# Wide attention: weights split inside the dense stage, normalisation moved into its own block; two order edits in the narrow attention

## The chip, the cores and the metric

The kernel runs on one core of a Trainium2 chip. The metric is the device time of one launch in microseconds. Three timed runs of the kernel before gave 2533.31, 2536.18 and 2537.85 us; their median is 2536.18 us. The engines are PE (TensorE, matmuls and transposes), DVE (VectorE), ACT (ScalarE), POOL (GpSimd) and SP (SyncE, which here only issues DMAs). Each engine executes its own instruction stream in order and meets the others at semaphores.

## The reference, cut to what matters

The program is a chain of eight sub-layers on `x` (16 batches, 112 tokens, 256 channels) with a context of 375 tokens per batch. Each one normalises the rows and adds its result to `x`: narrow attention (16 heads of 16), a top-1 expert layer, linear attention, a dense mixture of 8 small experts, **wide attention** (16 heads of 64), a top-2 expert layer, narrow attention again, a last expert layer. The layernorm and the wide attention, sub-layer 4, in essence:

```python
xn = (x - mean(x)) / sqrt(var(x) + 1e-5)             # over the 256 channels
q = xn @ Wq                                           # 256 -> 16 heads x 64
k, v = ctx @ Wk, ctx @ Wv                             # 375 context tokens
s = (q k^T) / sqrt(64), masked by the context mask
y = softmax(s) v                                      # per head
x = x + (y @ Wo + bo)
```

`k` and `v` depend on the context and the weights alone, `q` on the normalised rows.

## The kernel before, in words

Each sub-layer is a phase. A phase has one or more blocks; a block gives each engine its own instruction list, and all engines meet at the block's end. When a phase gives back its memory object (`Mem`, L31), its semaphores are cleared and there is a barrier of all engines (L39 to L43).

**Precision.** Most matmuls are made in three fp16 products (`PARTS`, L25): each operand is a high part (a cast of the value) and a low part (value minus high part). ACT makes the high parts; DVE or POOL the low ones. "Splitting" below means making both.

**Layernorm** (`layernorm_phase`, L91 to L206) is a block of its own. For four groups of four batches, DVE makes statistics (`bn_stats`, `bn_aggr`), ACT the root, DVE the reciprocal and the shift; ACT normalises rows 0 to 9, DVE rows 10 to 15; PE transposes (32 transposes, 112 x 128) into eight banks; ACT and DVE copy to `XT`, the transposed rows. Its SP list can fetch something for the next block (`fetch`), its POOL list can prepare something (`prepare`).

**Dense stage** (`dense_ffn_phase`, L1615 to L1874). After the routing, 32 units (8 experts x 4 groups of batches) follow. Per unit PE makes 12 output matmuls (L1844) and 6 hidden matmuls (L1824) of the unit four further on; ACT makes the gelu (L1725) and the high part of the hidden values (L1730), POOL the low part (L1686), DVE four additions to X (L1808). At every fourth unit ACT and DVE also split the weights of an expert (L1695, L1696, L1752, L1755). The output banks are four, one per batch of the group, and PE waits before each for the addition of the unit before.

**Wide attention** (`wide_attention_phase`, L209 to L649). Its layernorm's SP list fetches `Wk`, the context of batch 0, `Wq`, `Wv`, the context of batch 1, two masks, `Wo` and the bias (L287 to L296), into the room that the values use later (`staged`). Its POOL list splits `Wk` in three operations on 128 x 2048 (`prepare`, L298 to L304). After the layernorm's end a second block begins. Its lists start with a prologue: ACT makes the high parts of context 0, `Wq`, the rows of group 0, `Wv`, context 1 (L433 to L438), DVE the low parts of `Wq`, the rows, `Wv` (L527 to L533), POOL the low parts of the contexts and two masks (L356 to L360). Then come steps s from -3 to 132. Step s scores head pair s (L609), turns the weights of pair s - 2 (L619) and weighs the values of pair s - 3 (L635); 128 pairs in all. Between these lie the projection units of a step (`units_at`): keys `k` (6 matmuls, L572), queries `q` (L579), values `v` (L586), outputs (L595). They go through two banks in turn; a unit waits until the one two before it was emptied by DVE (L566). Steps -3 to -1 hold k, q and v units of batch 0; scoring starts at step 0.

**Narrow attention** (`narrow_attention_phase`, L652 to L1100), used by sub-layers 0 and 6; only in sub-layer 6 are there `v` units. All its projection units share ONE bank, so each waits until the one before was emptied (L1062). Per batch of 8 steps there are k (2), v (3), the turn of the maxima, `turn_y` (L1093, emptied by a reciprocal and a multiplication on DVE, L967 and L969), `turn_n` (L1096) and `out`. `units_at` (L666) lists the units of a step by batch. So in the step where `turn_y` of batch b and the second v unit of batch b + 2 meet, `turn_y` comes first. The SP list issues per batch the stacked keys, the maxima (L820), the context, and for each group of four batches the stacked queries (L813) at steps 8b - 20 and 8b - 12.

## Time and profile before

| what | value |
|---|---|
| timed runs, median | 2536.18 us |
| profiled execution, its own time | 2536.97 us |
| its span in the trace | 2535.3 us |
| mean granted clock of PE over the span | 0.921 |
| PE busy | 2168.5 us, 86% |
| DVE, ACT, POOL busy | 62%, 55%, 38% |

The trace's times begin at the span's start. The profiled execution's own time is 1.67 us above its span, and 0.79 us above the median of the timed runs. A row of a timeline begins with its start and its length in microseconds; the square bracket at its end is the idle time of that engine before it and the instruction that ended it.

### The profile page before, as it was taken

How to read it: one execution, taken by the hardware profiler on the slowest of the kernel's cores; microseconds unless marked ns; L12 is line 12 of the kernel's file. 1: busy time of each engine (PE TensorE's matmuls, PEld its weight loads, DVE VectorE, ACT ScalarE, POOL GpSimd, SP SyncE). 2: the span in 40 equal slices, each digit the busy share in tenths (PEclk: the TensorE clock that was granted, in tenths of full speed). 3: DMA queues.
4: the chain of work that ended last, by engine and by line, in shares of the span. 5: the costliest groups of instructions: out<-in, count | busy, mean ns of one | idle time of the engine just before them, and what ended most of it. 6: DMA issues, size and time to landing. Idle time of an engine off the chain costs nothing. (4 is left out here: it accounts for less than half of the span.)

```text
span 2535.3 us, 62742 instructions
## 1 busy us (share of the span) xinstructions
PE 2168.5 (86%) x24002; PEld 1469.8 (58%) x24002; DVE 1563.0 (62%) x3645; ACT 1402.4 (55%) x3000; POOL 969.5 (38%) x1069
## 2 busy tenths in 40 slices
PE   4999499599999999969699999999974975899755
PEld 2566256367777777747456666666652642566533
DVE  3667673576566556647777777777756544655463
ACT  3666563455555555535466666666654543666542
POOL 3553232154454445424423333333333733433143
PEclk8999699799999999989799999999987985999968
DMA  5663361400000000010200000000023233332133
GB/s 124 122 115 75 101 233 38 128 14 14 14 8 14 14 14 2 2 35 1 96 7 15 9 15 14 9 15 8 2 86 107 74 94 95 85 75 70 42 102 111
DMA packets 118583, 139.60 MB, mean 55 GB/s; under 512 B 15073, under 2 KB 107185, under 8 KB 118289
## 3 DMA queue, kind: packets, MB, share of 16 engines
q1 hardware_dynamic: 110900, 115.39, 17.6%
q0 software_dynamic: 7392, 20.19, 2.5%
q8 instruction: 200, 3.28, 0.5%
q14 instruction: 91, 0.74, 0.1%
HBM read 93.25 MB, written 17.47 MB: 44 GB/s over the span
## 5 line engine op out<-in xcount | busy, mean ns | idle before, releaser
L952 DVE TENSOR_REDUCE a_mx<-a_pair 112x2 f32<-112x750 f32 x256 | 238.0, 937 | 191.1 <-PE a_pair L1021 191.1
L1260 POOL TENSOR_TENSOR a_kp<-a_kp 125x512 f16<-125x512 f32 x192 | 217.6, 1157 | 259.4 <-ACT a_kp L1351 259.4
L353 POOL TENSOR_SCALAR a_P<-a_P,a_inv 112x375 f32<-112x375 f32 x256 | 148.4, 593 | 379.6 <-DVE a_inv L484 379.6
L391 ACT ACTIVATE a_P<-a_masked,a_least 112x375 f32<-112x375 f32 x256 | 153.4, 600 | 141.0 <-DVE a_least L479 141.0
L890 ACT ACTIVATE a_PT<-a_pair 125x672 f32<-125x672 f32 x256 | 186.2, 730 | 65.3 <-PE a_pair L1033 60.9
L479 DVE CUSTOM_DVE_ANT_0 a_masked<-a_s,a_mask_add 112x375 f32<-112x375 f32 x256 | 130.2, 547 | 81.7 <-PE a_s L609 79.4
L1394 DVE SCALAR_TENSOR_TENSOR a_k<-a_p,a_k 128x375 f16<-128x375 f32 x128 | 69.3, 547 | 139.2 <-ACT a_k L1307 139.1
L1351 ACT CAST a_kp<-a_kp 125x512 f16<-125x512 f32 x192 | 110.3, 617 | 76.9 <-DVE a_kp L1413 76.9
L572 PE MATMUL a_p<-a_kc,a_wk 128*128 128x375 f16 x768 | 146.2, 326 | 4.3 <-POOL a_kc L347 4.3
L586 PE MATMUL a_p<-a_wv,a_kc 128*125 128x512 f16 x576 | 144.6, 387 | 5.2 <-DVE a_v L518 3.7
L1493 PE MATMUL a_p<-a_kc,a_wk 128*128 128x375 f16 x768 | 142.2, 327 | 6.3 <-POOL a_kc L1252 6.3
L1493 PE MATMUL a_p<-a_wv,a_kc 128*125 128x512 f16 x576 | 141.0, 385 | 0.0
L2327 PE MATMUL f_hb<-w_w1h,f_x 128*128 x588 | 135.7, 367 | 0.0
L2415 ACT ACTIVATE all_XT<-f_hb 128x512 f32<-128x512 f32 (+1 forms) x98 | 53.1, 550 | 138.8 <-PE f_hb L2327 130.5
L1413 DVE TENSOR_SCALAR a_kp<-a_p 125x512 f32<-125x512 f32 x192 | 122.8, 682 | 8.1 <-PE a_p L1524 8.1
L619 PE MATMUL a_t<-all_ident,a_P 112*125 112x112 f32 x768 | 116.4, 288 | 3.4 <-POOL a_P L353 3.4
L489 DVE TENSOR_TENSOR a_PT<-a_t,a_PT 125x336 f16<-125x336 f32 x256 | 116.8, 498 | 2.6 <-ACT a_PT L427 2.6
L619 PEld LDWEIGHTS a_t<-all_ident,a_P 112*125 112x125 f32 x768 | 93.7, 188 | 38.9 <-issue 34.6
L586 PEld LDWEIGHTS a_p<-a_wv,a_kc 128*125 128x125 f16 x576 | 71.4, 137 | 61.4 <-DVE a_v L518 15.3
L1052 PE MATMUL a_y<-a_PT,a_values 125*32 125x112 f32 x3072 | 101.5, 265 | 5.3 <-ACT a_PT L890 5.3
L1403 DVE SCALAR_TENSOR_TENSOR a_v<-a_p,a_v 125x512 f16<-125x512 f32 x96 | 66.6, 694 | 58.4 <-ACT a_v L1318 56.8
L1033 PE MATMUL a_pair<-a_q,a_k 50*125 50x112 f16 (+1 forms) x1536 | 89.0, 223 | 15.0 <-DVE a_mx L952 8.6
(450 smaller groups left out, 5366.7 us busy)
## 6 DMA issues: line engine op xcount, KB each, us to landing
a_kc<-in_ctxT SPq DMA_DIRECT2D x64, 375.0 KB, 3.6
a_k<-a_k_parts SPq DMA_DIRECT2D x192, 93.8 KB
w_stage<-in_L_ffn_W SPq DMA_DIRECT2D x32, 512.0 KB
w_stage<-in_L_ffn_ew SPq DMA_DIRECT2D x16, 512.0 KB, 6.9
w_stage<-expert_rows SPq DMA_DIRECT2D x16, 448.0 KB, 8.1
a_v_in_sb<-in_ctx SPq DMA_DIRECT2D x16, 375.0 KB
a_q<-a_q_parts SPq DMA_DIRECT2D x48, 112.0 KB, 4.6
w_stage<-in_L_ffn_W SPq DMA_DIRECT2D x16, 256.0 KB, 4.5
```

Of the source, the lines that this page charges most:

```text
L353: pool.tensor_scalar(P[:, p % 4, r, :], P[:, p % 4, r, :], inv[:, p % 4, r:r + 1], 1.0, ALU.mult, ALU.mult).then_inc(P_done, 1)
L391: act.activation(P[:, p % 4, r, :], masked[:, p % 2, r, :], ACT.Exp, bias=least[:, p % 4, r:r + 1], scale=-1.0, accum_out=total[:, p % 4, ...
L479: dve.tensor_tensor_reduce(masked[:, p % 2, r, :], s_bank[0:S, r, 0:SK], mask_add[:, b % 2, :], 1.0, 3e38, ALU.add, ALU.min, least[:, p % ...
L572: mm = pe.matmul(out[:, 0:SK], wk16[:, z, j, c * 128:(c + 1) * 128], kc16[:, b % 2, x, j, :], start=i == j == 0, stop=(i, j) == (2, DC - 1))
L586: mm = pe.matmul(out[0:KP, 0:512], kc16[:, b % 2, x, j, jk * KP:(jk + 1) * KP], wv16[:, z, j, w * 512:(w + 1) * 512], start=i == j == 0, s ...
L619: mm = pe.transpose(t_bank[0:KP, r, j * S:(j + 1) * S], P[:, p % 4, r, j * KP:(j + 1) * KP], ident[0:S, 0:S])
L890: act.activation(PT[:, p % 4, :, :], pair_bank[slot["turned", p]][0:KP, :, 0:KT * S], ACT.Exp).then_inc(exp_done, 1)
L952: dve.tensor_reduce(mx[:, b % 2, 2 * pair:2 * pair + 2], pair_bank[slot["score", p]][0:S, :, 0:SK], AX.X, ALU.max).then_inc(max_done, 1)
L1260: pool.tensor_tensor(kp16[:, LO, j, hf, r, :, :].rearrange("p c m -> p (c m)"), kp[:, n % 4, :], kp16[:, HI, j, hf, r, :, :].rearrange("p ...
L1413: dve.tensor_scalar(kp[:, n % 4, :], p_bank[bank][0:KP, 0:512], 0.0, EPS * WS, ALU.max, ALU.add).then_inc(f_evac, 1)
L1493: mm = pe.matmul(out, lhs(x, z, j), rhs(x, z, j), start=i == j == 0, stop=(i, j) == (2, DC - 1))
L2327: mm = pe.matmul(bank[:, 0:BW], x16[:, j % 2, x, c, :], w.w1h[:, z, c, bass.ds(e, 1), cols].rearrange("p o f -> p (o f)"), start=False, st ...
```

## The change

- A new class `WideWeights` holds the wide attention's weight and context tiles. It is made before the dense stage, and the dense stage's second block has an SP list that issues their five DMAs. From unit 6 to unit 17 of the dense stage, ACT makes one high part and DVE one low part per unit, each 128 x 512 (12 pieces: three matrices, two chunks, two halves). At units 20 and 22 they split the contexts of batches 0 and 1.
- The wide attention has no layernorm block any more, and POOL's `prepare` and the prologue on POOL, ACT and DVE for weights and contexts are gone. A class `Normalised` carries out the layernorm within the block's steps, which now start at -9: keys 0, 1, 2 of batch 0 are projected at steps -9, -8, -7, values at -6, -5, -4, queries at -3, -2, -1. ACT normalises groups 0 and 1, DVE groups 2 and 3. The transposes use the score, turn and value banks. SP issues the masks, `Wo` and the bias at the block's start.
- Narrow attention: v units come first in their step; the stacked queries are issued at steps 8b - 22 and 8b - 14.
- There is one block less in the program, and as many `Mem` objects with semaphores as before; one is now given back at the end of the wide attention.

```diff
+class Normalised:
+    def statistics(self, dve, g):
+        for b in range(g * GT, (g + 1) * GT):
+            dve.bn_stats(self.stats[:, b, :], self.X[:, b, :]).then_inc(self.stats_done, 1)
...
+    def normalise_dve(self, dve, g):
+        dve.wait_ge(self.rstd_done, g + 1)
+        for b in range(g * GT, (g + 1) * GT):
+            dve.tensor_scalar(self.xn[:, b, :], self.X[:, b, :], self.mean_var[:, b, 0:1], self.rstd[:, b:b + 1],
+                              ALU.subtract, ALU.mult).then_inc(self.dve_rows, 1)
...
+    def normalise_act(self, act, g):
+        act.wait_ge(self.shift_done, g + 1)
...
+    def take_act(self, act, g, c, place):
+        act.wait_ge(self.turned, place + 1)
+        act.copy(self.XT[:, c, g * GW:(g + 1) * GW], self.banks[g][c][:, 0:GW]).then_inc(self.act_taken, 1)
+    def turn(self, pe, g, rows_done, count):
+        pe.wait_ge(rows_done, count)
+        for c in range(DC):
+            for t in range(GT):
+                mm = pe.transpose(self.banks[g][c][:, t * S:(t + 1) * S], self.xn[:, g * GT + t, c * 128:(c + 1) * 128],
+                                  self.ident[0:S, 0:S])
+            mm.then_inc(self.turned, 1)
...
+class WideWeights:
+    PIECES = [(w, c, h) for w in ("k", "q", "v") for c in range(DC) for h in range(2)]
...
+    def fetch(self, sp):
+        for w in ("k", "q", "v"):
+            sp.dma_start(self.staged[w], chunked(self.given[w])).then_inc(self.w_in[w], 16)
+        for b in range(2):
+            self.load_context(sp, b)
+    def high(self, act, i):
+        w, c, h = self.PIECES[i]
+        cols = slice(h * 512, (h + 1) * 512)
+        act.wait_ge(self.w_in[w], 16)
+        act.mul(self.w16[w][:, HI, c, cols], self.staged[w][:, c, cols], WS).then_inc(self.w_hi, 1)
+    def low(self, dve, i):
...
+        dve.wait_ge(self.w_hi, i + 1)
+        dve.scalar_tensor_tensor(self.w16[w][:, LO, c, cols], self.staged[w][:, c, cols], WS, self.w16[w][:, HI, c, cols],
+                                 ALU.mult, ALU.subtract).then_inc(self.w_split, 1)
...
# wide attention
-    FIRST, LAST = -3, NPAIR + WEIGH + 1
+    FIRST, LAST = -9, NPAIR + WEIGH + 1
-    V_FIRST = {-3: (0, 0), -1: (1, 0), 1: (2, 0), 2: (0, 1), 3: (1, 1), 4: (2, 1)}
+    K_FIRST = {-9: 0, -8: 1, -7: 2}
+    V_FIRST = {-6: (0, 0), -5: (1, 0), -4: (2, 0), 2: (0, 1), 3: (1, 1), 4: (2, 1)}
...
-        layernorm_phase(nc, tag + "n", X, XT, ident, fetch=fetch, prepare=prepare)
...
# ACT's list, before the units of step s
+                    if s == -8:
+                        norm.root(act, 0)
+                    if s == -7:
+                        norm.root(act, 1)
+                        norm.normalise_act(act, 0)
+                    if s == -6:
+                        norm.root(act, 2)
+                        norm.normalise_act(act, 1)
+                        norm.root(act, 3)
+                        for c in range(DC):
+                            norm.take_act(act, 0, c, c)
+                        high_x(0)
+                    if s == -4:
+                        for c in range(DC):
+                            norm.take_act(act, 1, c, DC + c)
+                    if s == -2:
+                        norm.take_act(act, 2, 0, 2 * DC)
+                    if s == -1:
+                        norm.take_act(act, 3, 0, 3 * DC)
...
# DVE's list, before the emptying of step s - 1's last unit
+                    if -8 <= s <= -6:
+                        g = s + 9
+                        norm.statistics(dve, g)
+                        norm.invert(dve, g - 1)
+                        norm.aggregate(dve, g)
+                        norm.shifts(dve, g - 1)
+                    if s == -5:
+                        norm.normalise_dve(dve, 2)
+                        low_x(0)
+                    if s == -4:
+                        norm.invert(dve, 3)
+                        norm.normalise_dve(dve, 3)
+                    if s == -2:
+                        norm.take_dve(dve, 2, 1, 2 * DC + 1)
+                    if s == -1:
+                        norm.take_dve(dve, 3, 1, 3 * DC + 1)
...
# PE's list, before the units of step s
+                    if s == -5:
+                        norm.turn(pe, 0, norm.act_rows, GT)
+                    if s == -4:
+                        norm.turn(pe, 1, norm.act_rows, 2 * GT)
+                    if s == -3:
+                        norm.turn(pe, 2, norm.dve_rows, GT)
+                    if s == -2:
+                        pe.wait_ge(norm.act_taken, 4)
+                        norm.turn(pe, 3, norm.dve_rows, 2 * GT)
...
# narrow attention
-        return found
+        return [u for u in found if u[0] == "v"] + [u for u in found if u[0] != "v"]
...
-                        if t in (-20, -12) and b % GT == 0:
-                            stack_queries(b // GT, (t + 20) // 8)
+                        if t in (-22, -14) and b % GT == 0:
+                            stack_queries(b // GT, (t + 22) // 8)
...
# dense stage, ACT and DVE at unit n
+                    if 6 <= n < 6 + len(following.PIECES):
+                        following.high(act, n - 6)
+                    if n in CONTEXT_AT:
+                        following.high_context(act, CONTEXT_AT.index(n))
...
+                    if kind == "unit" and 6 <= n < 6 + len(following.PIECES):
+                        following.low(dve, n - 6)
+                    if kind == "unit" and n in CONTEXT_AT:
+                        following.low_context(dve, CONTEXT_AT.index(n))
```

## Rows read from the trace of the kernel before

**Rows 1.** The page's parts 1 and 2: PE's share of the span, and its granted clock.

```profile
PE 2168.5 (86%) x24002; PEld 1469.8 (58%) x24002; DVE 1563.0 (62%) x3645; ACT 1402.4 (55%) x3000; POOL 969.5 (38%) x1069
...
PEclk8999699799999999989799999999987985999968
```

**Rows 2.** Busy us of engines by stretch: dense units, layernorm, prologue, steps; `PEclk` is the clock.

```profile
1146.00:1229.00 83.00, 81.46 (x592) 63.66 (x590) 62.26 (x154) 37.24 (x69) 34.05 (x30) 0.98 0.00 1
1229.00:1251.00 22.00, 9.30 (x32) 5.58 (x32) 20.08 (x48) 10.26 (x22) 11.34 (x3) 0.57 0.68 236
1251.00:1272.00 21.00, 14.52 (x55) 6.32 (x56) 11.11 (x10) 10.09 (x13) 7.40 (x4) 0.64 0.13 41
1272.00:1860.00 588.00, 579.69 (x5627) 380.53 (x5626) 432.30 (x1210) 399.81 (x1068) 197.62 (x300) 1.00 0.04 10
```

**Rows 3.** Timeline of PE from the prologue to step 0.

```profile
1254.15 2.04 PE L572 MATMUL a_p<-a_kc,a_wk 128*128 128x375 f16 x6 [4.27 <-POOL a_kc L347]
...
1267.55 1.14 PE L572 MATMUL a_p<-a_kc,a_wk 128*128 128x375 f16 x6
...
1271.36 0.69 PE L609 MATMUL a_s<-a_k,a_q 64*112 64x375 f16 x6
...
```

**Rows 4.** Timeline of DVE over the same stretch.

```profile
1214.75 1.66 DVE L1808 SCALAR_TENSOR_TENSOR all_X<-f_o,f_scaled,all_X 112x256 f32<-112x256 f32 x4 [0.79 <-PE f_o L1844]
...
1229.64 1.41 DVE L126 BATCH_NORM_STATS2 a4n_stats<-all_X 112x6 f32<-112x256 f32 x4
...
1239.62 3.89 DVE L145 TENSOR_SCALAR a4n_xn<-all_X,a4n_mean_var,a4n_rstd 112x256 f32<-112x256 f32 x2
...
1254.16 2.56 DVE L528 SCALAR_TENSOR_TENSOR a_wq<-a_v,a_wq 128x2048 f16<-128x2048 f32 x1 [3.62 <-ACT a_wq L435]
1256.65 1.08 DVE L468 TENSOR_TENSOR a_x<-all_XT,a_x 128x896 f16<-128x896 f32 x1
...
```

**Rows 5.** Timeline of ACT and of POOL over the same stretch.

```profile
1233.40 2.06 ACT L168 ACTIVATE a4n_xn<-all_X,a4n_shift,a4n_rstd 112x256 f32<-112x256 f32 x4
...
1252.22 1.91 ACT L435 ACTIVATE a_wq<-a_v 128x2048 f16<-128x2048 f32 x1
...
1209.09 1.55 POOL L1686 TENSOR_TENSOR f_h<-f_h 128x448 f16<-128x448 f32 x1 [1.41 <-ACT f_h L1730]
...
1236.02 5.39 POOL L300 TENSOR_SCALAR a_v<-a_v 128x2048 f32<-128x2048 f32 x1 [11.22 <-DMA a_v<-in_L_xattn_Wk]
...
```

**Rows 6.** DVE's groups in the dense stage's layernorm: count, busy us, mean ns.

```profile
L145 DVE TENSOR_SCALAR f3n_xn<-all_X,f_mean_var,f_rstd 112x256 f32<-112x256 f32 x6 | 2.1, 410 | 0.0
L131 DVE BATCH_NORM_AGGREGATE f_mean_var<-f3n_stats 112x2 f32<-112x6 f32 x16 | 1.5, 157 | 0.0
```

**Rows 7.** Timelines of DVE and POOL at the head of the dense stage.

```profile
1128.19 1.82 DVE L1752 SCALAR_TENSOR_TENSOR f_w1h<-f_w,f_w1h 128x256 f16<-128x256 f32 x1 [0.95 <-ACT f_w1h L1695]
...
1127.85 7.96 POOL L1682 TENSOR_TENSOR f_x<-all_XT,f_x 128x896 f16<-128x896 f32 x4 [22.94 <-ACT f_x L1692]
```

**Rows 8.** DVE at two phase ends: the last bracket is the gap between phases.

```profile
1870.61 0.06 DVE L148 MEMSET q5n_eps<- 112x1 f32 x1 [1.28 <-PEq L43]
...
2101.92 0.06 DVE L148 MEMSET a6n_eps<- 112x1 f32 x1 [2.57 <-PEq L43]
```

**Rows 9.** Timeline of PE in sub-layer 6: turn_y, the v unit behind it, and a q unit.

```profile
2255.63 0.65 PE L1093 MATMUL a_p<-all_ident,a_y_sb 128*112 128x128 f32 x4
2257.11 0.87 PE L1082 MATMUL a_p<-a_wv,a_kc 128*125 128x256 f16 x6 [0.83 <-DVE a_yn L969]
...
2266.28 1.77 PE L1076 MATMUL a_p<-all_XT,a_wq 128*128 128x448 f32 x4 [0.47 <-ACT a_values L918]
...
```

**Rows 10.** Waits of sub-layer 6: us in total, times, longest.

```profile
PE a_p L1082 <- DVE a_yn L969: 11.7, 14, 0.8
```

**Rows 11.** Timeline of SP's queue in sub-layer 6: context, then queries.

```profile
2235.51 0.40 SPq L735 DMA_DIRECT2D a_kc<-in_ctxT  x1
2236.01 2.75 SPq L813 DMA_DIRECT2D a_q<-a_q_parts  x3
...
```

More of the change, by code:

```diff
@@ L211, in wide_attention_phase @@
+def wide_attention_phase(nc, tag, X, XT, ident, given, Wo, bo, mask):
     HD, NP = 64, H // 2
@@ L226, in units_at @@
             t = s - NP * b
-            found += [("k", b, t + 3)] if 0 <= t + 3 < C else []
+            if b == 0:
+                found += [("k", 0, K_FIRST[t])] if t in K_FIRST else [("k", 0, t + 3)] if 0 <= t < C - 3 else []
+            else:
+                found += [("k", b, t + 3)] if 0 <= t + 3 < C else []
             if b == 0:
@@ L326, in _ @@
             def _(sp):
+                for b in range(2):
+                    load_mask(sp, b)
+                sp.dma_start(wo, chunked(Wo)).then_inc(rest_in, 16)
+                sp.dma_start(bo_bc[:, :], bo.unsqueeze(0).to_broadcast([S, D])).then_inc(rest_in, 16)
                 for s in steps:
@@ L331, in _ @@
                             sp.wait_ge(kc_split, b - 1)
-                            load_context(sp, b)
+                            given.load_context(sp, b)
                         if t == -12:
@@ L567, in project @@
                     if kind == "k":
-                        pe.wait_ge(wk_split, 1)
+                        pe.wait_ge(given.w_split, 4)
                         pe.wait_ge(kc_split, b + 1)
@@ L606, in score @@
                         pe.wait_ge(least_done, 2 * p)
+                    else:
+                        pe.wait_ge(norm.act_taken, 2)
                     for i, (x, z) in enumerate(PARTS):
@@ L617, in turn @@
                             pe.wait_ge(PT_done, 2 * (p - 1) + r + 1)
+                        else:
+                            pe.wait_ge(norm.act_taken, 6)
+                            pe.wait_ge(norm.dve_taken, 2)
                         for j in range(KT):
@@ L1677, in dense_ffn_phase, with _ @@
         with nc.Block() as block:
+            @block.sync
+            def _(sp):
+                following.fetch(sp)
             @block.gpsimd
@@ L2684, in sub7, with sub34 @@
                        a["L3_ffn_Wg"], bias=a["L3_ffn_bg"], out=out)
+        def sub34():
+            with ExitStack() as st2:
+                wide = WideWeights(Mem(nc, st2, "w4"), a["ctxT"], a["L2_xattn_Wq"], a["L2_xattn_Wk"], a["L2_xattn_Wv"])
+                sub3(wide)
+                sub4(wide)
         first_sub, stop = stop if isinstance(stop, tuple) else (0, stop)
-        for sub in (sub0, sub1, sub2, sub3, sub4, sub5, sub6, sub7)[first_sub:stop]:
+        for sub in (sub0, sub1, sub2, sub34, sub5, sub6, sub7)[first_sub:stop]:
             sub()
```

139 lines of the change are left out of this document (83 added, 56 removed).

## The prediction

> **What bounds the kernel now.** I read the page first, then a table by stretch, then the timelines of each engine between the dense stage and the wide attention. PE is busy for 86% of the span, and the page's slices show its clock at 9 or more nearly everywhere except at a few phase changes [rows 1]. The table shows which these are: in the dense units PE works 81.46 of 83 us at a clock of 0.98 and in the wide steps 579.69 of 588 us at 1.00, but between them lie 43 us with PE busy for 9.30 of 22 and 14.52 of 21 us, at 0.57 and 0.64, that is mostly at the lower of its two levels, 1.2 and not 2.4 GHz [rows 2]. So the change can win nothing in the steady steps except by taking work out of them; it can win in the 43 us, and it pays in the dense units, where PE is the bound as well.
>
> What fills the 43 us: the layernorm begins at 1229.64 [rows 4] and the first score comes at 1271.36 [rows 3], 41.7 us later. In the layernorm DVE is the late engine (20.08 busy of 22 us [rows 2]): two normalisations took 3.89 us [rows 4] where the same six took 2.1 us together, 0.35 each, in the dense stage's layernorm, in which POOL did nothing [rows 6]. Beside the slow ones POOL worked 5.39 us on Wk [rows 5]. Then the prologue: PE waits 4.27 us for a context's low part before its first key unit [rows 3], and DVE spends 2.56 us on Wq after waiting 3.62 us for its high part, the same again on Wv, and 1.08 us on the rows [rows 4].
>
> **The lead-in, step by step.** Call the new block's start 0; it is at 1229.6, as before, if the dense stage ends when it did. Keys and values need no row of x, so PE starts at once. DVE's list decides until step -4. Statistics take 1.41 us per group [rows 4] and aggregates 1.5 / 4 = 0.38 [rows 6], 7.2 us for four groups; three key units are emptied between them (0.5 each, from 2.56 us for 2048 columns [rows 4]), and reciprocals and shifts add some 0.4: 9.1 us. Group 2 is normalised in 4 x 0.35 [rows 6]: 10.5. The low part of the rows comes next and needs, in a row, eight transposes, two copies and a high part on ACT. ACT has normalised groups 0 and 1 by about 9 us (2.06 us each [rows 5], the second after DVE's second shift at 6.2); the chain then puts the high part at 11 to 13.5 and the low part (1.08 [rows 4]) at 12.2 to 14.5. A value unit, group 3 and another value unit on DVE (0.65 + 1.4 + 0.65) give 15 to 17. After that PE has two transposes of groups and three query units, each waiting for the unit two before.
>
> PE itself has 3 key, 3 value and 3 query units and four groups of transposes. At the low clock a key unit takes 2.04 us, at the high one 1.14 [rows 3]; by columns a query unit is 2.44 or 1.36, a value unit 2.79 or 1.56; a group of transposes is 9.30 / 4 = 2.3 us at the low clock [rows 2], half of it at the high. The sum is 31 us at the low clock and 16.5 at the high. So the first score is at about 21 if PE stays fast (DVE and the handovers are the bound) and at 31 if it stays slow (PE is). At the low clock PE would have no gaps, and in the prologue of before it went from 2.04 to 1.14 us for the same unit after a few us without gaps [rows 3]. I take 23, near the fast end. The gain is 41.7 - 23 = 18.7 us, with ends 10.7 and 20.7.
>
> At the first score all of before's lead-in units are done, and one value unit more (the third, step 1 before). It leaves the steps where PE is the bound: 6 products by the column rule, 1.5 us, less some overlap: 1.4.
>
> **The dense units.** A unit lasts 1.66 + 0.79 = 2.45 us, of which DVE is idle 0.79 [rows 4]. A low piece of 512 columns is a quarter of the 2.56 us for 2048 [rows 4], about 0.68 with its fixed part, so it fits: 1.66 + 0.68 = 2.34. At units 6, 10 and 14 the expert's weights are split too (about 0.8); DVE falls behind by 0.7 each and recovers 0.1 per unit, at most 1.7 us. PE waits for an addition only when it comes to the same bank again, a unit later, which leaves 1.5 to 2 us. ACT's high piece is a quarter of 1.91 us [rows 5], 0.5 to 0.6, on an engine that works 37.24 of 83 us [rows 2]. The DMAs are issued some 35 us before unit 6; nothing else loads in that stage (1 GB/s, the last column of [rows 2]). Taken: 0.5 us lost, with ends 0 and 15. The far end is for DVE and POOL holding each other up. At the stage's head one 256-wide DVE split, with both inputs in SBUF, took 1.82 us while POOL's operations ran, 7.96 us for four [rows 7]. In the units it went the other way: DVE's split began first, and POOL's low part, next to it, took 1.55 us [rows 5], which PE does not feel, as that unit's output is 1 to 2 units away. New pieces stand at the place of those splits, right behind the additions, so I take the cheap order.
>
> The Trainium skill (SBUF — State Buffer, section "SBUF: two separate sides") says that DVE with two SBUF inputs and GpSimd share one port pair, that whoever starts first keeps it for the whole instruction, and that the other blocks. Both rows agree. By that rule the dense stage is a lottery of some 0.1 us in starts; if POOL won each time, the far end holds (it is a rival below).
>
> **The ends of phases.** One gap between blocks goes with the layernorm; it is inside the 41.7 us. One more memory object is given back at the wide attention's end. A phase end with one such object shows a gap of 1.28 us, one with three 2.57 [rows 8]: 0.65 each. Taken: +0.65, ends 0.3 and 1.3.
>
> **Narrow attention.** In sub-layer 6 PE waits 14 times 0.83 us, 11.7 in all, between turn_y and the value unit behind it, as both use the one bank and DVE must first take its two steps [rows 9, 10]. With the value unit first, turn_y waits for ACT instead; that handover shows 0.47 us before a query unit [rows 9]. DVE's two steps then lie beside the score, the turned score and the weighing of the next step, over 1 us of PE's work, before turn_n asks for them. 14 x (0.83 - 0.47) = 5.0 us; at the last two or three batches DVE's maxima are late as well, so 4.6, with ends 0 and 6. Sub-layer 0 has no value units. The queries: SP issues them directly behind the context anyway (2235.51, 2236.01 [rows 11]), so moving them up two steps mostly swaps these two. What is queued behind them on SP, the keys, is not ready then, and the context is wanted ten steps later. Where they wait for a free buffer SP waits longer, but no longer than to the same point. Taken: 0, within 1 either way.
>
> **The sum.** -18.7 - 1.4 + 0.5 + 0.65 - 4.6 = -23.6 us. From the profiled execution's own time, 2536.97, that gives 2513.4; on the scale of the median, 0.8 lower, 2512.6. I predict 2513.
>
> **Rivals.**
> 1. *PE stays slow in the lead-in.* For: the clock is at its lower level in the layernorm and until some 37 us after its start [rows 2, 3], and new gaps between units could keep it there. Against: at that level there are no gaps. First score at 31: 8 us less won, 2521. Chance 0.13.
> 2. *POOL wins the port in the dense units.* Each of 12 pieces then costs 1.0 us more, 1.66 + 0.68 + 1.03 (POOL's length without a wait: 1.55 less half a us) - 2.45 = 0.9, with weights and contexts 15: 2527. Chance 0.07. If each piece is held for as long as at the stage's head (1.82 for 256 columns [rows 7], so 2.1 for 512), it is 12 x (1.66 + 2.1 - 2.45) = 16, the six weight splits 6 x 1.4 = 8, two contexts 5: 29 lost in place of 0.5, and the kernel is slower, 2541. It decides from 24 us lost. Against: beside the split in the units it was POOL that was held, not DVE [rows 5]. Chance 0.03.
> 3. *The narrow order wins nothing*, because ACT's handover comes behind an exponential, or the maxima become the bound: 2518. Chance 0.15.
> 4. *More is won*: the lead-in ends at 20, DVE's chain loses its handovers, narrow gives 6: 2507. Chance 0.12.
> The forecast has the other 0.50.
>
> **How the numbers follow.** All but the slow branch of the second are faster by more than 5 us, which is the 0.2% that this kernel's measurement can tell. Range: 2505 to 2523 takes in the first, third and fourth, and leaves out 2527 and 2541 and the tails. Faster 0.95, within 0.2% 0.02, slower 0.03.
>
> **What would show it.** The first score should come 21 to 25 us after the dense stage's end gap, key units at once, DVE without pieces over 2 us in the statistics. The dense units should keep 2.45 us, with no PE idle on DVE's additions beyond 1 us. In sub-layer 6 the 0.83 us waits should be gone and 14 of about 0.47 us stand before turn_y; the wait in front of turn_n should not appear. The steps of the wide attention keep their pace. Wrong would be: PE at 2.04 us per key unit up to step 0; unit lengths of 3 us from unit 6 to 17; a new wait of a maximum in sub-layer 6.

## The result, and the profile after

The changed kernel takes 2510.47 us (median of 4 runs, 2509.68 to 2512.50) where the kernel before takes 2536.11 (4 runs, 2533.31 to 2537.85). The ratio is 0.9896, with a 95% interval of 0.9881 to 0.9911: 26 us faster, between 23 and 30. The prediction said 2513, in a range from 2505 to 2523. The profiled execution took 2512.50 us, with a span of 2510.8, 24.5 less than before's 2535.3.

The page's parts 1 and 2 after, against [rows 1]: PE, DVE and POOL are busy for 8 to 10 us less. The 20th digit of the clock, the slice that holds the lead-in of the wide attention, is 9 where it was 7.

```profile
PE 2160.3 (86%) x24002; PEld 1468.2 (58%) x24002; DVE 1554.1 (62%) x3659; ACT 1403.2 (56%) x3008; POOL 959.8 (38%) x1064
...
PEclk8899789899999999988999999999986995999867
```

**Where the time went.** I cut the trace at the first instruction of each sub-layer's layernorm (DVE's memset of `eps`) and measured the stages, here for before, after and the whole-program kernels of the experiments below. In us:

```
                       sub 0   sub 1   sub 2  dense 3  wide 4   sub 5   sub 6   sub 7    span
before                 260.6   213.6   625.7   118.4   641.0   231.3   297.9   135.5   2535.3
after                  267.9   213.7   625.2   118.5   618.0   228.5   292.3   135.3   2510.8
changed_again          262.6   212.7   627.6   117.1   619.0   232.3   290.5   133.0   2506.8
e1_old_queries         259.3   211.9   625.4   118.5   618.0   227.8   291.7   120.2   2484.6
e2_old_values          268.0   213.8   625.2   118.5   617.9   228.6   296.4   120.7   2500.6
e3_narrow_only         267.8   211.4   625.7   118.4   642.0   230.3   293.6   121.1   2521.6
e4_wide_only           261.8   212.1   627.3   117.0   618.9   228.0   296.5   122.0   2495.5
e5_dense_split         260.2   212.3   627.5   117.1   625.3   230.8   294.4   120.6   2499.8
e7_pool_first          268.7   213.3   624.6   117.8   618.1   228.1   296.6   134.5   2513.6
e8_context_first       269.1   212.7   627.5   117.1   619.0   227.8   291.9   135.6   2512.3
e9_context_late        267.9   214.9   625.4   118.9   618.3   228.7   292.3   133.0   2510.7
```

After minus before: the wide attention -23.0, sub-layer 6 -5.6, sub-layer 5 (no code changed) -2.8, **sub-layer 0 +7.3**, the other four -0.5 together. The table tells also what one profile is worth: sub-layers 1, 2 and 5, whose code is the same in every kernel, spread by 3 to 4.5 us (sub-layer 5: 227.8 to 232.3). The wide stage with its new lead-in agrees within 1.1 us (617.9 to 619.0). One of the 12 runs of e3_narrow_only took 2552.92 us at a granted clock of 0.879 and stands in none of its figures below.

**The lead-in.** Engines by stretch after, against [rows 2]: dense units, the lead-in's two halves, steps. The columns are those of [rows 2].

```profile
1153.00:1236.00 83.00, 81.47 (x592) 63.71 (x590) 70.42 (x168) 44.78 (x83) 42.96 (x31) 0.98 0.00 1
1236.70:1246.60 9.90, 6.81 (x33) 4.01 (x34) 9.75 (x46) 7.80 (x18) 2.35 (x2) 0.83 0.66 214
1246.60:1256.50 9.90, 8.59 (x57) 5.60 (x57) 6.65 (x13) 6.02 (x12) 0.00 (x0) 1.00 0.00 1
1256.50:1845.00 588.50, 580.26 (x5631) 381.48 (x5631) 432.55 (x1211) 400.02 (x1067) 197.61 (x300) 1.00 0.04 10
```

The 43 us of before with PE at 0.57 and 0.64 are now 19.8 us. In the first half DVE is busy for 9.75 of 9.90 us, so it is the bound there; in the second half it is PE, at full clock. PE's timeline, against [rows 3]:

```profile
1236.82 2.09 PE L720 MATMUL a_p<-w_kc,w_wk 128*128 128x375 f16 x12 [2.35 <-PEq L43]
...
1240.79 1.14 PE L720 MATMUL a_p<-w_kc,w_wk 128*128 128x375 f16 x6 [1.88 <-DVE a_k L645]
1243.02 2.82 PE L734 MATMUL a_p<-w_wv,w_kc 128*125 128x512 f16 x6 [1.09 <-DVE a_k L645]
...
1246.53 1.46 PE L734 MATMUL a_p<-w_wv,w_kc 128*125 128x512 f16 x6
...
1250.06 1.51 PE L734 MATMUL a_p<-w_wv,w_kc 128*125 128x512 f16 x6 [1.31 <-DVE w_v L654]
...
1254.08 2.44 PE L727 MATMUL a_p<-a_x,w_wq 128*128 128x448 f16 x12
1256.45 0.69 PE L759 MATMUL a_s<-a_k,a_q 64*112 64x375 f16 x6
```

Two key units take 2.09 us together right at the block's start, the high level (1.14 for one in [rows 3]); only one value unit, 2.82 against 1.46, ran at the low level; and PE's idle brackets name DVE's emptying. DVE's timeline, against [rows 4]:

```profile
1236.70 1.41 DVE L231 BATCH_NORM_STATS2 a_stats<-all_X 112x6 f32<-112x256 f32 x4
...
1245.11 1.37 DVE L254 TENSOR_SCALAR a_space<-all_X,a_mean_var,a_rstd 112x256 f32<-112x256 f32 x4
...
1248.31 1.09 DVE L604 TENSOR_TENSOR a_x<-all_XT,a_x 128x896 f16<-128x896 f32 x1 [1.83 <-ACT a_x L506]
...
1250.13 1.38 DVE L254 TENSOR_SCALAR a_space<-all_X,a_mean_var,a_rstd 112x256 f32<-112x256 f32 x4
```

The block begins at 1236.70 and the first score is at 1256.45: 19.75 us, where before took 41.7. Four normalisations take 1.37 us, 0.34 each, where two had taken 3.89 beside POOL. In before that row has two neighbours that were slow as well, while POOL worked on Wk: a shift that takes 0.13 us here, and four more normalisations.

```profile
1236.63 3.07 DVE L139 SCALAR_TENSOR_TENSOR a4n_shift<-a4n_mean_var,a4n_rstd 112x4 f32<-112x4 f32 x1
...
1243.64 4.99 DVE L145 TENSOR_SCALAR a4n_xn<-all_X,a4n_mean_var,a4n_rstd 112x256 f32<-112x256 f32 x4
```

From the first score to the next layernorm's memset it is 598.20 us, where before had 1870.61 - 1271.36 = 599.25.

**The dense units.** DVE and then POOL around unit 6, against [rows 4, 5]:

```profile
1177.21 0.42 DVE L1926 SCALAR_TENSOR_TENSOR f_w2h<-f_w,f_w2h 128x256 f16<-128x256 f32 x1
1177.55 0.69 DVE L335 SCALAR_TENSOR_TENSOR w_wk<-w_v,w_wk 128x512 f16<-128x512 f32 x1
1178.15 1.66 DVE L1979 SCALAR_TENSOR_TENSOR all_X<-f_o,f_scaled,all_X 112x256 f32<-112x256 f32 x4
...
1185.08 1.66 DVE L1979 SCALAR_TENSOR_TENSOR all_X<-f_o,f_scaled,all_X 112x256 f32<-112x256 f32 x4 [0.19 <-PE f_o L2019]
```

```profile
1176.98 2.15 POOL L1853 TENSOR_TENSOR f_h<-f_h 128x448 f16<-128x448 f32 x1 [1.41 <-ACT f_h L1897]
...
1179.43 1.88 POOL L1853 TENSOR_TENSOR f_h<-f_h 128x448 f16<-128x448 f32 x1 [0.29 <-ACT f_h L1897]
```

DVE's piece takes 0.69 us; it is POOL's low part that is held, 2.15 us in this unit and 1.88, 1.60 and 1.48 in the next three. The same four lengths come back, within 0.01 us, in the units from 10 and from 14. PE's only wait for DVE from 1150 to 1236 us was this one (us in total, times, longest), and the stage kept its length, 118.4 to 118.5.

```profile
PE f_o L2016 <- DVE f_gT L1967: 1.3, 1, 1.3
```

**The end of the wide phase,** against the first of [rows 8]: the gap with one more object given back is 1.75 us for 1.28. The second gap of [rows 8], where nothing was changed, is 2.1 us after for 2.57 before, so a single gap tells the price of an object only within half a us.

```profile
1854.65 0.06 DVE L148 MEMSET q5n_eps<- 112x1 f32 x1 [1.75 <-PEq L43]
```

**Sub-layer 6.** The wait of [rows 10] is gone. In its place (first fence: waits), and on PE's timeline, against [rows 9]:

```profile
PE a_p L1255 <- ACT a_values L1080: 6.6, 14, 0.5
```

```profile
2233.67 0.87 PE L1244 MATMUL a_p<-a_wv,a_kc 128*125 128x256 f16 x6
2235.02 0.65 PE L1255 MATMUL a_p<-all_ident,a_y_sb 128*112 128x128 f32 x4 [0.48 <-ACT a_values L1080]
2236.06 0.78 PE L1214 MATMUL a_y<-a_PT,a_values 125*32 125x112 f32 x24
2236.77 0.41 PE L1258 MATMUL a_p<-all_ident,a_yn 112*128 112x112 f32 x2
```

14 waits of 0.83 us became 14 of 0.47, and turn_n follows with no wait before it.

**Sub-layer 0.** This is where the profile contradicts the prediction. SP's queue, first before, then after (start, us to issue):

```profile
116.62 0.29 SPq L738 DMA_DIRECT2D a_v_in_sb<-in_ctx  x1
116.95 0.54 SPq L735 DMA_DIRECT2D a_kc<-in_ctxT  x1
119.11 1.89 SPq L813 DMA_DIRECT2D a_q<-a_q_parts  x3
...
```

```profile
122.71 0.29 SPq L900 DMA_DIRECT2D a_v_in_sb<-in_ctx  x1
125.19 1.88 SPq L975 DMA_DIRECT2D a_q<-a_q_parts  x3
127.11 1.80 SPq L897 DMA_DIRECT2D a_kc<-in_ctxT  x1
129.01 3.79 SPq L962 DMA_DIRECT2D a_k<-a_k_parts  x6
```

The queries issue no earlier than they did: 2.49 us after the values (`v_in_sb`) before, 2.48 after, because SP waits 2.1 us for their free buffer (L973). The context, now behind them, comes 4.40 us after the values and not 0.33, so it is 4.1 us late. Of the sub-layer's six pairs two are so; in the other four the context is 1.9 to 2.0 us late, the time that the queries take to issue.

PE's waits for the maxima, which come over the same queue, in the sub-layer before and after:

```profile
PE a_pair L1033 <- DMA a_q<-a_mT: 6.3, 5, 2.0
```

```profile
PE a_pair L1195 <- DMA a_q<-a_mT: 10.5, 6, 3.4
```

4.2 us more stand in that line. They can't be the whole account of the 7.3: PE is also busy for 219.9 us in this stage where it was 215.4, with the same 2992 matmuls, at a granted clock of 0.89 for 0.92. Whether the moved queries did it, and by how much, a single pair of profiles can't say; most of the experiments are about that.

### The profile page after: what moved, and what is told of

The parts are those of the page before. It is cut to its first block and busy times, and to the rows that moved or that the text cites. A ratio compares the mean times of both kernels' runs of the same rounds, so it can differ in the third digit from the quotient of the medians.

```text
span 2510.8 us, 62752 instructions
## 1 busy us (share of the span) xinstructions
PE 2160.3 (86%) x24002; PEld 1468.2 (58%) x24002; DVE 1554.1 (62%) x3659; ACT 1403.2 (56%) x3008; POOL 959.8 (38%) x1064
## 5 line engine op out<-in xcount | busy, mean ns | idle before, releaser
L475 POOL TENSOR_SCALAR a_space<-a_space,a_inv 112x375 f32<-112x375 f32 x256 | 148.4, 593 | 384.0 <-DVE a_inv L620 384.0
L513 ACT ACTIVATE a_space<-a_space,a_least 112x375 f32<-112x375 f32 x256 | 153.4, 600 | 141.1 <-DVE a_least L615 141.1
L615 DVE CUSTOM_DVE_ANT_0 a_space<-a_s,a_mask_add 112x375 f32<-112x375 f32 x256 | 130.2, 547 | 81.7 <-PE a_s L759 79.3
L734 PE MATMUL a_p<-w_wv,w_kc 128*125 128x512 f16 x576 | 144.6, 387 | 6.1 <-DVE w_v L654 5.0
L720 PE MATMUL a_p<-w_kc,w_wk 128*128 128x375 f16 x768 | 144.3, 323 | 4.2 <-PEq L43 2.3
L1655 PE MATMUL a_p<-a_kc,a_wk 128*128 128x375 f16 x768 | 142.2, 326 | 6.3 <-POOL a_kc L1414 6.3
L1655 PE MATMUL a_p<-a_wv,a_kc 128*125 128x512 f16 x576 | 141.0, 385 | 0.0
L2502 PE MATMUL f_hb<-w_w1h,f_x 128*128 x588 | 135.6, 367 | 0.0
L772 PE MATMUL a_t<-all_ident,a_space 112*125 112x112 f32 x768 | 116.3, 288 | 3.4 <-POOL a_space L475 3.4
L772 PEld LDWEIGHTS a_t<-all_ident,a_space 112*125 112x125 f32 x768 | 93.5, 188 | 38.9 <-issue 34.3
L734 PEld LDWEIGHTS a_p<-w_wv,w_kc 128*125 128x125 f16 x576 | 71.3, 137 | 61.7 <-DVE w_v L654 16.8
```

The costliest lines, as they stand in the source:

```text
L475: pool.tensor_scalar(P[:, p % 4, r, :], P[:, p % 4, r, :], inv[:, p % 4, r:r + 1], 1.0, ALU.mult, ALU.mult).then_inc(P_done, 1)
L513: act.activation(P[:, p % 4, r, :], masked[:, p % 2, r, :], ACT.Exp, bias=least[:, p % 4, r:r + 1], scale=-1.0, accum_out=total[:, p % 4, ...
L615: dve.tensor_tensor_reduce(masked[:, p % 2, r, :], s_bank[0:S, r, 0:SK], mask_add[:, b % 2, :], 1.0, 3e38, ALU.add, ALU.min, least[:, p % ...
L720: mm = pe.matmul(out[:, 0:SK], wk16[:, z, j, c * 128:(c + 1) * 128], kc16[:, b % 2, x, j, :], start=i == j == 0, stop=(i, j) == (2, DC - 1))
L734: mm = pe.matmul(out[0:KP, 0:512], kc16[:, b % 2, x, j, jk * KP:(jk + 1) * KP], wv16[:, z, j, w * 512:(w + 1) * 512], start=i == j == 0, s ...
L772: mm = pe.transpose(t_bank[0:KP, r, j * S:(j + 1) * S], P[:, p % 4, r, j * KP:(j + 1) * KP], ident[0:S, 0:S])
```

## The experiments

Each kernel was timed beside the kernel before on the same chip, and ratios are to it. Absolute times differ from chip to chip (below), so they are compared only among kernels timed together.

### One part at a time

**The changed kernel with the queries back at their old steps:**

```diff
-                        if t in (-22, -14) and b % GT == 0:
-                            stack_queries(b // GT, (t + 22) // 8)
+                        if t in (-20, -12) and b % GT == 0:
+                            stack_queries(b // GT, (t + 20) // 8)
```

> The changed kernel with the stacked queries issued at steps 8b - 20 and 8b - 12 again. Sub-layer 0, from the start of its layernorm (11.4) to that of the next, took 260.6 us in the kernel before and 267.9 in the changed one, though only this edit touches it. Theory A, the moved queries cost it: they go ahead of a context and push what follows on SP's queue, the maxima land later. Then sub-layer 0 is back at about 261 us and the kernel at about 2504. Rival B, the landing of the DMAs varies from one execution to the next: sub-layer 0 lies anywhere in 260 to 268 here, and the kernel is at 2510 within 2 us.

Measured: 2491.06 us (2486.35 to 2497.59), before 2525.98; ratio 0.9874 (0.9851 to 0.9897). Sub-layer 0 took 259.3 us, sub-layer 6 291.7.

**The changed kernel with the value units back in their old order:**

```diff
-        return [u for u in found if u[0] == "v"] + [u for u in found if u[0] != "v"]
+        return found
```

> The changed kernel with the units of a narrow step in their old order (values not first), queries moved. Theory: PE waits 14 times 0.83 us behind turn_y again; sub-layer 6, 292.3 us in the changed kernel from its layernorm's start to the next one's, takes 297 to 298, and the kernel 2515 to 2516. Rival: the 5.6 us came from the moved queries or from chance, and the kernel stays at 2510 to 2511. Sub-layer 0, by theory A of the first run, is at about 268, by B anywhere in 260 to 268.

Measured: 2505.34 us (2497.90 to 2507.65); ratio 0.9920 (0.9899 to 0.9942). Sub-layer 6 took 296.4 us, sub-layer 0 268.0.

**Before with both narrow edits and nothing else** (the two diffs above turned round, on the kernel before):

> The kernel before with both edits of the narrow attention and none of the wide. By the prediction's terms it gains 4.6 us: 2531.5. By the traces, sub-layer 6 gains 5.6 and, by theory A, sub-layer 0 loses 7: 2537 to 2538. By rival B sub-layer 0 is unchanged on the mean: 2530.5.

Measured: 2523.80 us (2520.68 to 2528.70); ratio 1.0008 (0.9986 to 1.0031), between 4 us faster and 8 slower. The 4.6 us that the prediction's terms give are outside, though sub-layer 6 took 293.6 us in place of 297.9. Sub-layer 0 took 267.8.

**The wide attention's and the dense stage's edits alone** (both narrow edits undone, as in the two diffs):

> The changed kernel with both narrow edits undone: the wide and dense edits alone. By the prediction's terms 19.0 us faster than before, 2517. By the traces, where the stretch from the wide layernorm's start to the next layernorm went from 641.0 to 618.0 us and the dense stage stayed (118.4 and 118.5), 23 us: 2513. Both narrow parts together are then this kernel less the changed one: 2 to 3 us if the 23 hold, 6 to 7 if the 19 do.

Measured: 2497.95 us (2493.79 to 2503.21); ratio 0.9895 (0.9873 to 0.9916). Wide stage 618.9 us, dense 117.0.

What follows from the four, all from one chip: by the medians the wide and dense edits give 28.0 us, the value order 6.9 (2497.95 - 2491.06), and the moved queries cost 7.4 (2505.34 - 2497.95). By the ratios it is 26.5, 5.3 and 6.3. The last two have intervals of about 8 us each way, so only their signs are suggested. The value order has a better measure in the table: sub-layer 6 took 292.0 us in the mean of the six profiles that have it (290.5 to 293.6) and 296.4 in the five that don't (294.4 to 297.9), 4.3 less. And it shows that the queries do nothing in sub-layer 6: 291.7 with the old steps, 292.3 and 290.5 with the new.

### Why moved queries should cost anything

Two kernels were meant to tell the early queries from the late context. **Queries moved, but behind the context of the same step:**

```diff
                         if t == -11:
                             stack_keys(b)
-                        if t in (-22, -14) and b % GT == 0:
-                            stack_queries(b // GT, (t + 22) // 8)
...
                             load_context(sp, b)
+                    for b in range(0, B, GT):
+                        t = s - 8 * b
+                        if t in (-22, -14):
+                            stack_queries(b // GT, (t + 22) // 8)
```

> The changed kernel with the queries still at steps 8b - 22 and 8b - 14, but behind the context of the same step on SP's queue. Sub-layer 0 took 267.8 to 268.0 us in the three kernels with the queries moved and 259.3 to 261.8 in the three without. Theory C: the harm is that the moved queries stand ahead of a context, which then comes late and is moved when the maxima want to land. Then sub-layer 0 is back at 260 to 262 us and the kernel 7 us below the changed one. Rival D: the early queries themselves crowd the DMA queues behind the maxima; sub-layer 0 stays at 268.

Measured: 2511.21 us (2505.24 to 2518.28), before 2539.80; ratio 0.9894 (0.9858 to 0.9929). Sub-layer 0 took 269.1 us, as the rival had it and not the theory.

**Old query steps, the context at 8b - 28, behind them:**

```diff
-                        if t in (-22, -14) and b % GT == 0:
-                            stack_queries(b // GT, (t + 22) // 8)
+                        if t in (-20, -12) and b % GT == 0:
+                            stack_queries(b // GT, (t + 20) // 8)
...
-                        if t == -30 and b >= 3:
+                        if t == -28 and b >= 3:
```

> The changed kernel with the queries at their old steps and the context two steps later (8b - 28), so that it stands behind them on SP's queue and ahead of the keys. Theory C: a late context alone does the harm, sub-layer 0 at 267 to 268 us. Rival D: the queries are where they were, sub-layer 0 at 260 to 262.

Measured: 2514.19 us (2512.43 to 2520.29); ratio 0.9916 (0.9886 to 0.9945). Sub-layer 0 took 267.9 us.

**The changed kernel itself, on the same chip:**

> The changed kernel itself, as the reference on the same chip for the other kernels: sub-layer 0 at 268 us, the stretch from the wide attention's start to the next layernorm at 618, sub-layer 6 at 292, 1.0 to 1.1% faster than before.

Measured: 2509.12 us (2508.52 to 2510.25); ratio 0.9889 (0.9862 to 0.9916). Sub-layer 0 took 262.6 us here, where the same kernel had taken 267.9.

**These two kernels can't tell theory C from rival D.** A step is a place in SP's list and not a time: SP issues its list in order and waits only for what each entry needs. The context stands at steps 8b - 30, and no entry lies between it and the queries' old place two steps on. So "queries moved, but behind the context" is the list with the old query steps over again, entry by entry, and "old query steps, context later" is the changed kernel's. SP's queue in the first shows it, 2.16 us from the context to the queries as in before:

```profile
119.43 0.55 SPq L897 DMA_DIRECT2D a_kc<-in_ctxT  x1
121.59 1.89 SPq L975 DMA_DIRECT2D a_q<-a_q_parts  x3
```

The intervals of the three kernels overlap. What the two are good for is repetition. With the old order sub-layer 0 took 260.6, 259.3, 261.8, 260.2, 268.7 and 269.1 us (before, e1, e4, e5, e7, e8), with the new one 267.9, 262.6, 268.0, 267.8 and 267.9 (after, changed_again, e2, e3, e9): means of 263.3 and 266.8, and either order with short and long passes. A single profile of sub-layer 0 tells nothing of an effect below 8 us. So the sub-layer was repeated.

**Sub-layer 0 six times over, and nothing else of the program but the first load and the last store of X**, in three versions: old query steps; moved; moved but behind the context, which by the above is the first over again. The other sub-layers are left out, so what these kernels write is not the program's output.

```diff
-        for sub in (sub0, sub1, sub2, sub34, sub5, sub6, sub7)[first_sub:stop]:
-            sub()
+        for i in range(6):
+            narrow_attention_phase(nc, "n" + "abcdef"[i], X, XT, ident, a["ctxT"], a["L0_WqT"], a["L0_WkT"], a["L0_WcT"],
+                                   a["L0_xattn_bc"], a["L0_bq"], a["L0_bk"], ctx=a["ctx_1024"])
...
```

> Sub-layer 0 alone, carried out six times in a row (weights and context of sub-layer 0 each time), and X written out; the other sub-layers are left out. Queries at the old steps 8b - 20 and 8b - 12. In whole kernels sub-layer 0 with the old steps took 260.6, 261.8, 259.3 and once 268.7 us, with the moved ones 267.8 to 269.1 and once 262.6, so one profile does not tell. Theory A (the moved queries cost 5 to 7 us per sub-layer): this kernel lies 30 to 42 us below the one with moved queries, near 1585 against 1620. Rival B (chance from one execution to the next): both within 6 us of each other, and single sub-layers in one profile spread over 259 to 269.

> The same six sub-layers with the queries at 8b - 22 and 8b - 14, ahead of the step's context. Theory A: six times 5 to 7 us more than with the old steps. Rival B: the same within 6 us.

> The same six sub-layers with the moved queries behind the context of their step. If it is the displaced context that costs (theory C), this lies at the kernel with the old steps; if the moved queries themselves (D), at the one with moved queries. By rival B all three agree within 6 us.

| version | median, us | from, to | ratio to before, interval |
|---|---|---|---|
| old steps | 1602.30 | 1595.10, 1610.17 | 0.6347 (0.6328 to 0.6365) |
| moved | 1619.28 | 1608.94, 1628.62 | 0.6413 (0.6389 to 0.6437) |
| moved, behind the context (the old order again) | 1602.31 | 1592.72, 1611.34 | 0.6339 (0.6318 to 0.6361) |

Six moved sub-layers cost 17 us (from the intervals of the ratios, 9 to 25), 2.8 us each (1.5 to 4). The first and the third version, which issue the same list, agree within 0.01 us in their medians; their ten runs lie between 1592.72 and 1611.34 us, those of the new order between 1608.94 and 1628.62, and only two of the ten are above the lowest of those six. So the edit's price is real, it comes of the exchange of context and queries on the queue, which is all that the edit does there, and it is less than half of the 7.3 us that the first profile showed. Whether the early queries or the late context cost it, no run tells.

By which instruction it makes itself felt stays open. The waits for the maxima, which had seemed to be it, come to 48.1 and 51.9 us over the six sub-layers in the profiles of the old order, and to 55.1 in that of the new; the largest of a single sub-layer is alike (old steps, moved):

```profile
PE na_pair L1195 <- DMA na_q<-na_mT: 10.7, 5, 4.0
```

```profile
PE nc_pair L1195 <- DMA nc_q<-nc_mT: 10.7, 5, 3.8
```

More stands in PE's busy time, for the same number of matmuls (old steps, moved, moved behind the context):

```profile
PE 1306.4 (82%) x17952; PEld 825.5 (52%) x17952; DVE 910.2 (57%) x1548; ACT 920.0 (58%) x1536; POOL 647.4 (41%) x793
```

```profile
PE 1318.8 (82%) x17952; PEld 834.9 (52%) x17952; DVE 910.8 (56%) x1548; ACT 920.8 (57%) x1536; POOL 647.7 (40%) x793
```

```profile
PE 1310.6 (82%) x17952; PEld 829.8 (52%) x17952; DVE 910.5 (57%) x1548; ACT 921.3 (57%) x1536; POOL 648.3 (40%) x793
```

The spans of these three profiles are 1596.5, 1613.9 and 1603.9 us, the granted clocks 0.888, 0.881 and 0.891. Of the 13.7 us between the moved version and the mean of the other two, 10.3 are PE's busy time. So the exchange seems to cost mainly by a lower clock and less by PE's waits, as far as one profile of each tells.

And equal sub-layers of one kernel differ by more than the effect: the second begins at 274.8 us in the profile of the version with the old steps, the third at 539.0, the fourth at 808.1, the fifth at 1066.4: 264.2, 269.1 and 258.3 us.

### The lead-in: splitting elsewhere, or normalising beside

**Weights split in the dense stage, but the layernorm in a block of its own and the steps from -3 as before** (the narrow edits undone):

```diff
-    FIRST, LAST = -9, NPAIR + WEIGH + 1
+    FIRST, LAST = -3, NPAIR + WEIGH + 1
-    K_FIRST = {-9: 0, -8: 1, -7: 2}
-    V_FIRST = {-6: (0, 0), -5: (1, 0), -4: (2, 0), 2: (0, 1), 3: (1, 1), 4: (2, 1)}
+    V_FIRST = {-3: (0, 0), -1: (1, 0), 1: (2, 0), 2: (0, 1), 3: (1, 1), 4: (2, 1)}
...
+        layernorm_phase(nc, tag + "n", X, XT, ident, fetch=fetch)
```

> Narrow edits undone; weights and contexts are split in the dense stage, but the wide attention keeps its own layernorm block (without POOL's work in it) and its steps from -3. It tells how the 22 us of the lead-in share out. Theory: the layernorm block takes 12.7 us as in the dense stage instead of 20.9, the prologue only the rows of group 0, so the first score comes some 26 us after the layernorm's start (41.7 before, 19.8 in the changed kernel): 15 to 16 us of the 22 belong to the split, 6 to 7 to the overlap. From the wide layernorm's start to the next one 624 to 626 us. Rival: the layernorm stays near 20 us also without POOL's work and the split alone brings under 10 us.

Measured: 2509.59 us (2501.51 to 2513.53), before 2526.66; ratio 0.9936 (0.9922 to 0.9949). The wide stage took 625.3 us, between 641.0 and 618.0. DVE's and then PE's timeline of this kernel:

```profile
1228.72 1.40 DVE L126 BATCH_NORM_STATS2 a4n_stats<-all_X 112x6 f32<-112x256 f32 x4
...
1235.76 0.73 DVE L145 TENSOR_SCALAR a4n_xn<-all_X,a4n_mean_var,a4n_rstd 112x256 f32<-112x256 f32 x2
```

```profile
1233.12 7.87 PE L204 MATMUL a4n_b<-all_ident,a4n_xn 112*128 112x112 f32 x32 [6.63 <-ACT a4n_xn L168]
1242.77 2.04 PE L677 MATMUL a_p<-w_kc,w_wk 128*128 128x375 f16 x6 [1.78 <-PEq L43]
...
1254.40 0.68 PE L714 MATMUL a_s<-a_k,a_q 64*112 64x375 f16 x6
```

From the layernorm's start to the first score it is 1254.40 - 1228.72 = 25.7 us: 16.0 of the 22.0 us won come from taking the splits out of the lead-in, 6 from laying the layernorm beside the projections. The pair of normalisations takes 0.73 us without POOL beside it, 3.89 with it [rows 4]. With the shift before it (0.13 us for 3.07) and the four behind it (1.38 for 4.99) these seven operations of DVE are 9.7 us shorter, so most of the 16.0 lies where DVE had worked beside POOL's splits of Wk. And here, with PE idle for 6.63 us first, the first key unit runs at 2.04 us, the low level.

### Who wins the port in the dense units

**The wide edits alone, and in units 6 to 17 DVE waits until POOL has been given its low part, so that POOL begins first;** two tiny memsets on DVE are added for the order:

```diff
                     if kind == "unit" and 6 <= n < 6 + len(following.PIECES):
+                        dve.wait_ge(h_hi, n + 4)
+                        for c in range(2):
+                            dve.memset(tick[:, n - 6, c, :], 0.0)
                         following.low(dve, n - 6)
```

> The kernel with the wide edits alone (narrow edits undone), and in units 6 to 17 of the dense stage DVE waits until POOL's low part has been released, makes two tiny memsets and only then its weight piece. So POOL starts first each time. By the rule of the shared port pair (second rival of the prediction) DVE is then held for POOL's 1.03 us before each of the 12 pieces: 1.66 + 0.2 + 1.03 + 0.68 = 3.6 us of DVE per unit against 2.45 of PE, 12 to 14 us more in the dense stage (118.4 to about 131 from its layernorm's start to the wide block's). If DVE is not held, DVE needs 2.6 us per unit and the stage gains 2 to 3 us (121).

Measured: 2513.71 us (2508.14 to 2515.30), before 2539.80; ratio 0.9898 (0.9869 to 0.9927). The dense stage kept its length, 117.8 us. DVE's pieces of 512 columns and POOL's low part in this kernel:

```profile
1176.47 1.48 DVE L335 SCALAR_TENSOR_TENSOR w_wk<-w_v,w_wk 128x512 f16<-128x512 f32 x1
...
1179.49 0.67 DVE L335 SCALAR_TENSOR_TENSOR w_wk<-w_v,w_wk 128x512 f16<-128x512 f32 x1
```

```profile
1175.85 1.54 POOL L1854 TENSOR_TENSOR f_h<-f_h 128x448 f16<-128x448 f32 x1 [1.41 <-ACT f_h L1898]
...
1178.30 1.04 POOL L1854 TENSOR_TENSOR f_h<-f_h 128x448 f16<-128x448 f32 x1 [0.90 <-ACT f_h L1898]
```

The first piece, begun after POOL's operation, took 1.48 us in place of 0.69; the second 0.67; six later ones 0.73 or 0.91. All 12 took 9.8 us, 8.2 in the changed kernel. So the hold in this direction exists, 0.8 us for one piece, but the experiment forced it in full only once: having fallen behind, DVE found its wait already met in the units after. So neither stage length that was expected, 131 us with the hold or 121 without, came out, and neither was tested over 12 units. What it shows is that one such hold doesn't reach PE.

## Why the prediction was right, and where a term was wrong

| term | predicted | measured |
|---|---|---|
| lead-in, to the first score | -18.7 (-10.7 to -20.7) | 41.7 to 19.75 us: -22.0 |
| value unit out of the steps | -1.4 | -1.5 (599.25 to 598.20, less the wider gap), with a spread of 1.1 between equal stages |
| one more object given back | +0.65 | +0.47 (1.28 to 1.75) |
| dense units | +0.5 (0 to 15) | +0.1 |
| value units first | -4.6 (0 to -6) | -4.3 over eleven profiles; -5.1 in the wait of the first |
| queries two steps earlier | 0 (within 1) | +2.8 (1.5 to 4) by repetition; sub-layer 0 +7.3 in the first profile |
| sub-layer 5, no code changed | none | -2.8, within its spread |
| sum | -23.6 | -24.5 in the span; -25.6 in the medians |

**The lead-in** came out by the mechanism given, and beyond the better end of its range. The step that was mis-sized is "I take 23, near the fast end": DVE's chain was the bound, as worked out (the rows' low part came 11.6 us after the start, where 12.2 to 14.5 was given), and PE did not start at the low level. The sum had left it room for slow units; only one was slow, and PE was busy for 15.4 us of the 19.8. (At the high level the sum given as 16.5 adds up to 16.8.) The lead-in's half of rival 4, an end at 20, is what happened. Rival 1 is refuted by the 2.09 us for two key units. The separate-block kernel splits the gain: 16.0 and 6. The prediction had not divided it.

**The dense units** went as in the cheap case of the port. 1.66 + 0.69 us fit in a unit, and PE worked 81.47 of 83 us as before. Rival 2 is against the trace: the pieces took 0.68 to 0.69 us, all twelve. POOL was the one held, by 1.1 us at worst (2.15 for 1.03), twice the 0.5 of [rows 5]; at that unit DVE had a weight split and a piece back to back (1177.21 and 1177.55), and units 10 and 14, which have the same splits, show the same 2.14 and 2.15, the others 1.48 to 1.88. In all twelve POOL's operation ended 0.9 us after the end of DVE's piece. The hold of DVE by POOL, 1.48 us for 0.69 in the experiment, agrees with the rule of the Trainium skill (SBUF — State Buffer, section "SBUF: two separate sides") that whoever starts first keeps the shared pair. Not all recorded starts do: at 1179.43 POOL's low part begins 0.29 us ahead of DVE's piece (1179.72, 0.68 us), and it is POOL that takes 1.88 us. What no run showed is a dense stage in which POOL wins every time, so rival 2's price of 15 us was not tried.

**The value order** was right in kind and size: 0.83 us became 0.47, 14 times, and no wait stands before turn_n. Rival 3 is refuted by the sub-layer's lengths.

**The queries are the term that failed.** The step was: "moving them up two steps mostly swaps these two ... the context is wanted ten steps later. Where they wait for a free buffer SP waits longer, but no longer than to the same point. Taken: 0". The swap was seen, and its price set at nothing from sub-layer 6's rows, where indeed it costs nothing (291.7 and 291.9 us against 292.3, 290.5 and 292.3). SP did wait to the same point, as written: the queries issued 2.48 us after the values where it had been 2.49. What the step left out is that the context now stands behind that wait and behind 1.9 us of issue, and comes 1.9 to 4.1 us later. And the edit acts on sub-layer 0 too, which no row of mine covered. There, in a sub-layer 30 us shorter, the exchange costs 2.8 us per pass, and in sub-layer 6 it wins nothing. The kernel thus gives back a good half of what the value order wins, and that fits the two narrow edits alone coming to nothing (1.0008).

**The total** was 2.5 us above the measured one. In the profiled pair the 3.3 us more from the lead-in, 1.0 more in sub-layer 6 and the 2.8 of sub-layer 5, which no code explains, stood against the 7.3 of sub-layer 0; so its closeness owes something to terms that cancelled.

**The better version** is the change without the queries' edit. Its order of issue was timed twice, 0.9874 (0.9851 to 0.9897) and 0.9894 (0.9858 to 0.9929) of before; that of the full change three times, 0.9896, 0.9889 and 0.9916. The intervals overlap; that it is the faster rests on the repeated sub-layer, not on them.

## What to carry to other kernels

Work that only waits for weights belongs in the stage before, if an engine there has slack per unit and its deadline is a unit or more away; most of the gain (16 of 22 us here) was in that, not in overlapping the normalisation. An edit in a function that two stages call is priced in both, and one that puts a transfer ahead of another on a queue is priced at the one that is displaced. When the effect is smaller than the spread of a stage between profiles, repeat the stage in one program rather than read one profile more closely: the 7.3 us became 2.8. And before a variant is called a test, write out the order in which each list issues: three of the kernels here had other step numbers and a list that was already there.

## What the runs showed of the hardware that was not expected

- Sub-layer 7, whose code is the same everywhere, took 120.2 to 122.0 us in the profiles of five kernels and 133.0 to 135.6 in those of the six others. The five came from chips on which the kernel before took 2525.98 and 2526.66 us, the others from where it took 2536.11 and 2539.80: 9 to 14 us apart as well. So it seems to go with the chip and not with the kernel; the cause stays open.
- Equal sub-layers in one execution differ by up to 15 us (256.1 and 270.8 in the third version of the repeated sub-layer), with no change in the code.
- PE kept its high level over an idle time of 2.35 us at a phase's end (two key units in 2.09 us behind it), after 83 us at 0.98, and fell for one unit 6 us later; where 6.63 us of idle time and transposes came before, the first key unit ran at the low one.
